# A graph network's edge stages: TensorE's results one or two steps further from their readers, and its semaphore increments moved from matmuls to drains

## The chip, the cores and the metric

The kernel runs on one core of one Trainium2 chip. The metric is the device time of one execution in microseconds (us). The core has five engines with a queue each: TensorE (PE: matmuls and the weight loads before them), VectorE (DVE), ScalarE (ACT), GpSimd (POOL, which here issues the gathers) and SyncE (SP, which issues the other DMAs). The engines meet through semaphores: an instruction adds to one, and another waits until it has reached a number.

## The reference

A node table of 12,500 rows of 128 floats, 200,000 edges with `src` (random) and `dst` (sorted), and 16 attributes for each edge. In short:

```
h  = relu(layernorm(x))
logit = tanh(h @ W1.T) @ w2                       # one number a node
x1 = x + segment_softmax_sum(logit[src], h[src])  # the pooling: softmax over the edges of each dst
h  = relu(layernorm(x1))
y  = relu(transformer_conv(h, 8 heads of 16))     # the multi-head stage
out = x1 + transformer_conv(y, 1 head of 128)     # the single-head stage
transformer_conv: q[dst] . (k[src] + edge_attr @ We), softmax over the edges of each dst,
                  sum of weight * (v[src] + edge_attr @ We), plus x @ Ws + bs
```

## The kernel before

The edges are cut into 391 blocks of 512 (four columns of 128), the nodes into 98 tiles of 128. An *item* is a block with one tile that its `dst` values touch; there are 488 items, since some blocks touch several tiles. Three edge stages run over all items, one after the other: "pool" (`dense_stage`, L1060), "multi" (`edge_stage`, L661) and "single" (`dense_stage` again). Between them are short stages over nodes.

In each edge stage GpSimd gathers the source rows of a block by four indirect DMAs (L1133, or L752 in multi) into a ring of blocks and waits until a slot has been read. Each other engine runs its own program, `step(n, u)` for n = 0, 1, ..., which `rolled` (L67) writes out in full. Within a step an engine works on items that lie back by a fixed number: `m1 = n - 1`, `m2 = n - 2` and so on. These numbers, the order of the pieces in each `step`, and the waits are all that sets the order of the work.

The chain of one item in the two dense stages, with the names of its semaphores: ScalarE copies the gathered rows out of the ring (`rows`); in single, TensorE turns them (`rowT`) and ScalarE copies the result (`rowT_sb`); TensorE makes the scores in PSUM (`score`); VectorE masks them and takes the running minimum (`low`); ScalarE makes `exp` of them (`prob`) and of the change of the minimum (`factor`); TensorE turns the probabilities (`probT`); VectorE copies them to SBUF (`probT_sb`); TensorE multiplies them with the rows (`partial`); VectorE adds that to the tile's sums (`summed`). In pool, TensorE also makes the edge terms of the multi stage for each of the 391 blocks (`term_made`), and ScalarE copies them (`term_copied`). Each of TensorE's results there has two PSUM buffers.

In multi, TensorE has seven groups of matmuls in each step, each with its semaphore: `alphaT` (L911), `partial` (L924 and L926), `prefix` (L931), `edge_max` (L937 and L939), `onehotT` (L945), `tile_max` (L953) and `query` (L962). The chain of one item passes TensorE three times in one step: `alphaT`, the scan on VectorE, `prefix`, `ends` on VectorE, `tile_max`.

Every group of matmuls ends in one increment, which hangs on its last matmul (`i.then_inc(...)`).

## Time and profile before

| | |
|---|---|
| median of 3 runs | 9990.61 us (9988.7 to 9993.93) |
| the profiled execution, first to last instruction | 10223.7 us |
| mean granted clock of TensorE in it | 0.744 |
| busy: PE, DVE, ACT, POOL | 67%, 45%, 35%, 45% |
| pool, multi, single | windows 213 to 3195, 3464 to 6790, 6917 to 10118 us |

The profiled execution is one of its own and 233 us (2.3%) longer than the median of the others. PE is the engine's matmuls, PEld its weight loads, which run beside matmuls. A granted clock of 1.0 means that TensorE ran at 2.4 GHz, 0.5 that it ran at 1.2 GHz; a number between is a mix over the stretch. The modelled end of a matmul in such a profile doesn't tell when its semaphore arrives: for that one reads when the waiting engine starts. "Remote" as the releaser of a wait means that no instruction of the profile ended within 1.5 us before the semaphore moved. The chain that ended last, in the page's own count, covers only the last node stage and tells nothing of the edge stages.

### The profile page before, as it was taken

To read this page: it belongs to the slowest core of one execution; us is meant where nothing else is said; L and a number is where in the kernel's file an instruction comes from. 1 tells how busy PE (TensorE), PEld (TensorE's weight loads), DVE (VectorE), ACT (ScalarE), POOL (GpSimd) and SP (SyncE) were. 2 spreads that over 40 slices of the span, in tenths; PEclk is the share of its full clock that TensorE was granted. 3 is DMA by queue.
4 is the path that set the end of the run, shared out by engine and by line. 5 is a ranking of instruction groups with operands and counts; after the bars stand their busy time and mean duration, and the time that the engine had idled before them with its cause. 6 is when DMAs were issued, how large, how long until landed. Compare 5 with 4: busy or idle time off the path is not lost. (4 is left out here: it accounts for less than half of the span.)

```text
span 10223.7 us, 177251 instructions
## 1 busy us (share of the span) xinstructions
PE 6865.3 (67%) x40779; PEld 5286.7 (52%) x40779; DVE 4586.4 (45%) x12423; ACT 3560.6 (35%) x8557; POOL 4600.9 (45%) x4738
## 2 busy tenths in 40 slices
PE   3667666687655555555566666676777778778787
PEld 2556656576544345555555555553444444444445
DVE  3233333333346555566666666662333333333333
ACT  2233333333323344444444444442222323233332
POOL 2555544444441355544444444425544444444441
PEclk6666667767777677777777777787777878888888
DMA  2333333343322544444444444443333333333332
GB/s 77 95 102 103 101 102 105 105 109 107 94 59 80 151 136 137 136 138 138 135 136 136 137 137 141 136 141 74 76 75 76 77 74 76 74 75 75 73 75 62
DMA packets 1085568, 1056.97 MB, mean 103 GB/s; under 512 B 398824, under 2 KB 857244, under 8 KB 1084532
## 3 DMA queue, kind: packets, MB, share of 16 engines
q1 hardware_dynamic: 909364, 633.73, 22.8%
q0 software_dynamic: 175168, 411.90, 15.6%
q8 instruction: 349, 5.72, 0.2%
q14 instruction: 687, 5.63, 0.2%
HBM read 885.97 MB, written 159.07 MB: 102 GB/s over the span
## 5 line engine op out<-in xcount | busy, mean ns | idle before, releaser
L752 POOL DMA_INDIRECT ring_multi<-kv_rows,src_cols x1564 | 1606.5, 1027 | 1766.8 <-DVE kv L837 1205.8
L1133 POOL DMA_INDIRECT ring_single<-h_rows,src_cols x1564 | 1476.4, 944 | 1688.9 <-ACT row_single L1301 1180.6
L1133 POOL DMA_INDIRECT ring_pool<-pool_rows,src_cols x1564 | 1476.6, 944 | 1609.7 <-ACT row_pool L1301 1000.8
L1262 PE MATMUL ps_p_pool<-row_pool,probT_pool 128*128 128x129 f32 x3904 | 798.3, 369 | 998.8 <-DVE probT_pool L1226 924.9
L1262 PEld LDWEIGHTS ps_p_pool<-row_pool,probT_pool 128*128 128x128 f32 x3904 | 707.5, 271 | 1074.9 <-DVE probT_pool L1226 990.3
L1306 ACT ACTIVATE rowT<-ps_r 128x512 f32<-128x512 f32 x488 | 291.3, 597 | 2190.6 <-remote 1216.2
L1242 PE MATMUL ps_s_single<-rowT,cols 128*128 128x512 f32 x976 | 657.1, 762 | 465.2 <-issue 393.4
L1262 PE MATMUL ps_p_single<-row_single,probT_single 128*128 128x145 f32 x3904 | 737.9, 344 | 219.0 <-DVE probT_single L1226 181.0
L1213 DVE CUSTOM_DVE_ANT_0 masked_single<-mask_single,ps_s_single,start_single 128x512 f32<-128x512 bf16 x488 | 364.9, 748 | 986.4 <-PE ps_s_single L1244 524.7
L1262 PEld LDWEIGHTS ps_p_single<-row_single,probT_single 128*128 128x128 f32 x3904 | 663.5, 238 | 248.1 <-DVE probT_single L1226 202.8
L924 PE MATMUL ps_p_multi<-message_multi,onehot 128*128 128x136 f32 x3904 | 751.6, 354 | 4.8 <-issue 4.8
L1213 DVE CUSTOM_DVE_ANT_0 masked_pool<-mask_pool,ps_s_pool,start_pool 128x512 f32<-128x512 bf16 x488 | 365.0, 748 | 831.9 <-remote 408.5
L931 PE MATMUL ps_f_multi<-ident,prefix_multi 36*128 36x36 f32 x488 | 136.7, 280 | 880.9 <-DVE prefix_multi L847 633.2
L924 PEld LDWEIGHTS ps_p_multi<-message_multi,onehot 128*128 128x128 f32 x3904 | 704.4, 262 | 4.2 <-issue 4.2
L1010 ACT ACTIVATE onehot<-onehot_multi 128x512 f32<-128x512 bf16 x488 | 307.3, 630 | 1139.7 <-remote 863.1
L1292 ACT ACTIVATE prob_pool<-masked_pool,low_pool 128x512 f32<-128x512 f32 x488 | 352.2, 722 | 939.1 <-DVE low_pool L1213 617.8
L837 DVE TENSOR_TENSOR kv<-ring_multi,term_multi 128x1024 f32<-128x1024 f32 x488 | 598.5, 1226 | 157.6 <-issue 149.4
L1244 PE MATMUL ps_s_single<-edge_tail,cols_tail 17*128 17x512 f32 x976 | 663.5, 764 | 0.0
L1312 ACT ACTIVATE edge_term<-ps_e_pool 128x512 f32<-128x512 f32 x391 | 231.4, 592 | 1111.4 <-remote 663.4
L1278 PE MATMUL ps_e_pool<-w_edge,attr_cols 16*128 16x128 f32 x3128 | 583.5, 339 | 10.2 <-DMA attr_cols<-in_edge_cols 10.2
L931 PEld LDWEIGHTS ps_f_multi<-ident,prefix_multi 36*128 36x128 f32 x488 | 75.7, 155 | 985.2 <-DVE prefix_multi L847 682.5
L1278 PEld LDWEIGHTS ps_e_pool<-w_edge,attr_cols 16*128 16x128 f32 x3128 | 495.7, 237 | 113.0 <-issue 113.0
(224 smaller groups left out, 13519.3 us busy)
## 6 DMA issues: line engine op xcount, KB each, us to landing
term_multi<-edge_terms SPq DMA_DIRECT2D x488, 256.0 KB
edge_terms<-edge_term SPq DMA_DIRECT2D x391, 256.0 KB
dst_pool<-in_dst_rows SPq DMA_DIRECT2D x488, 128.0 KB
dst_multi<-in_dst_rows SPq DMA_DIRECT2D x488, 128.0 KB
dst_single<-in_dst_rows SPq DMA_DIRECT2D x488, 128.0 KB
query_multi<-query_parts SPq DMA_DIRECT2D x488, 96.0 KB
cols<-query_cols SPq DMA_DIRECT2D x488, 64.0 KB
ring_pool<-pool_rows,src_cols POOLq DMA_INDIRECT x1564
```

What stands on the lines that cost most here:

```text
L752: pool.indirect_dma_start(out=ring[:, u, j, :], out_offset=None, in_=rows, in_offset=bass.IndirectOffsetOnAxis(ap=g.src_cols[:, c:c + 1], ...
L837: V.tensor_tensor(out=kv[:, u1 % 4], in0=in_ring(items.block(m1), 0, 2 * D).rearrange("p j (a c) -> p j a c", a=2), in1=term[:, m1 % EB].u ...
L924: T_.matmul(ps_p[:, 0:acc_w], lhs, rhs, start=(j == 0), stop=False)
L1010: S_.activation(onehot32[:, p3], onehot[:, m3 % OB], ACT.Copy).then_inc(E["onehot32"].sem, 1)
L1133: pool.indirect_dma_start(out=ring[:, u, j, :], out_offset=None, in_=rows, in_offset=bass.IndirectOffsetOnAxis(ap=g.src_cols[:, c:c + 1], ...
L1213: V.tensor_tensor_reduce(out=masked[:, p], in0=mask[:, p], in1=ps_s[p][:], scale=1.0, scalar=start[:, p], op0=ALU.add, op1=ALU.min, accum_ ...
L1242: T_.matmul(ps_s[p1][:], cols[:, u1 % QB], rowT[:, p1], start=True, stop=False)
L1244: T_.matmul(ps_s[p1][:], cols_tail[:, u1 % QB], edge_tail[:, u1], start=False, stop=True)\
L1262: i = T_.matmul(ps_p[p3][:, 0:acc_w], probT[:, p3, j], row[:, u3, j, 0:acc_w], start=(j == 0), stop=(j == J - 1))
L1278: i = T_.matmul(ps_e[n % 2][:, j * D:(j + 1) * D], attr[:, n % EB, j * P:(j + 1) * P], w_edge[:], start=True, stop=True)
L1292: S_.activation(prob[:, p2], masked[:, p2], ACT.Exp, bias=low[:, p2], scale=-1.0)\
L1306: S_.activation(rowT[:, u % 2], ps_r[u % 2][:], ACT.Copy).then_inc(E["rowT_sb"].sem, 1)
```

## The change

1. All increments of TensorE in the three edge stages leave the last matmul of their group and go to a `drain` instruction behind it. A drain waits in TensorE's queue until the engine has finished all that came before; then it increments.
2. In the pool stage the product `partial` moves from TensorE's step n - 3 to n - 5 and `probT` from n - 2 to n - 3; VectorE reads them at n - 4 and n - 2 instead of n - 2 and n - 1. In single, TensorE's pieces but `rowT` move one step further still (`late = 1`): `score` at n - 2, `probT` at n - 4, `partial` at n - 6, and ScalarE's `exp` at n - 3.
3. ScalarE copies the gathered rows one item ahead, ahead of its `exp`, and in single the turned rows one item back. `factor` has 8 buffers instead of 4.

The core of the diff; in multi the other six groups are changed as the one shown:

```diff
-                    T_.matmul(ps_p[:, 0:acc_w], g.ident[:], kept_sums[:, p5], start=False, stop=True)\
-                      .then_inc(E["partial"].sem, 1)
+                    T_.matmul(ps_p[:, 0:acc_w], g.ident[:], kept_sums[:, p5], start=False, stop=True)
+                    pe.drain().then_inc(E["partial"].sem, 1)
...
+    late = 1 if single else 0
...
-        factor = sb(g, ph, f"factor_{kind}", [P, 4, 1])
+        factor = sb(g, ph, f"factor_{kind}", [P, U, 1])
...
         @block.vector
-                m1, u1, p1 = n - 1, (u - 1) % U, (u - 1) % 2
-                m2, p2, f2 = n - 2, u % 2, (u - 2) % 4
+                m2, p2 = n - 2, u % 2
+                m4, p4, f4 = n - 4, u % 2, (u - 4) % U
...
+                if has(m4, ITEMS):
+                    E["partial"].wait(dve, m4)
+                    E["factor"].wait(dve, m4)
...
+                    E["probT"].wait(dve, m2)
+                    E["partial"].wait(dve, m2 - 2)
+                    V.tensor_copy(probT[:, p2].rearrange("p j n -> p (j n)"), ps_t[p2][:])\
...
         @block.tensor
-                m1, u1, p1 = n - 1, (u - 1) % U, (u - 1) % 2
-                m2, p2 = n - 2, u % 2
-                m3, u3, p3 = n - 3, (u - 3) % U, (u - 3) % 2
+                m1, u1, p1 = n - 1 - late, (u - 1 - late) % U, (u - 1 - late) % 2
+                m3, p3 = n - 3 - late, (u - 3 - late) % 2
+                m5, u5, p5 = n - 5 - late, (u - 5 - late) % U, (u - 5 - late) % 2
...
+                if has(m5, ITEMS):
+                    E["probT_sb"].wait(pe, m5)
+                    E["summed"].wait(pe, m5 - 2)
...
+                    pe.drain().then_inc(E["partial"].sem, 1)
                 if has(m3, ITEMS):
...
+                    E["prob"].wait(pe, m3)
+                    E["probT_sb"].wait(pe, m3 - 2)
...
+                    pe.drain().then_inc(E["probT"].sem, 1)
...
         @block.scalar
+                k, r = n + 1, n - 1
+                m2, p2, f2 = n - 2 - late, (u - 2 - late) % 2, (u - 2 - late) % U
...
+                if n == 0:
+                    rows_of_item(0, 0)
+                if has(k, ITEMS):
+                    rows_of_item(k, 1)
+                if single and has(r, ITEMS):
+                    E["rowT"].wait(act, r)
```

The distances show at the start of a stage, where the pieces come in one by one. TensorE at the start of the pool stage, before (`ps_e` is the edge terms, `ps_s` the scores, `ps_t` the turned probabilities, `ps_p` the product):

```order
L1278 MATMUL ps_e_pool<-w_edge,attr_cols 128x128 x4
L1249 MATMUL ps_s_pool<-ident,row_pool 128x128 x4
L1278 MATMUL ps_e_pool<-w_edge,attr_cols 128x128 x4
L1249 MATMUL ps_s_pool<-ident,row_pool 128x128 x4
L1269 MATMUL ps_t_pool<-ident,prob_pool 128x128 x4
L1278 MATMUL ps_e_pool<-w_edge,attr_cols 128x128 x4
L1249 MATMUL ps_s_pool<-ident,row_pool 128x128 x4
L1262 MATMUL ps_p_pool<-row_pool,probT_pool 128x129 x4
L1269 MATMUL ps_t_pool<-ident,prob_pool 128x128 x4
```

Two scores stand ahead of the first turn, and the first product comes one step behind that turn. The same place after the change:

```order
L1280 MATMUL ps_e_pool<-w_edge,attr_cols 128x128 x4
L1251 MATMUL ps_s_pool<-ident,row_pool 128x128 x4
L1280 MATMUL ps_e_pool<-w_edge,attr_cols 128x128 x4
L1251 MATMUL ps_s_pool<-ident,row_pool 128x128 x4
L1271 MATMUL ps_t_pool<-ident,prob_pool 128x128 x4
L1280 MATMUL ps_e_pool<-w_edge,attr_cols 128x128 x4
L1251 MATMUL ps_s_pool<-ident,row_pool 128x128 x4
L1271 MATMUL ps_t_pool<-ident,prob_pool 128x128 x4
L1280 MATMUL ps_e_pool<-w_edge,attr_cols 128x128 x4
L1251 MATMUL ps_s_pool<-ident,row_pool 128x128 x4
L1264 MATMUL ps_p_pool<-row_pool,probT_pool 128x129 x4
L1271 MATMUL ps_t_pool<-ident,prob_pool 128x128 x4
```

Three scores stand ahead of the first turn, and the first product comes two steps behind it; within a step, once all pieces run, the order is the old one. (Drains are not among such rows.) ScalarE at the start of the single stage, before (rows that only compute addresses stand between):

```order
L1301 ACTIVATE row_single<-ring_single 128x4x128
L1306 ACTIVATE rowT<-ps_r 128x512
L1292 ACTIVATE prob_single<-masked_single,low_single 128x512
L1295 ACTIVATE factor_single<-start_single,low_single 128x1
L1299 REGISTER_ALU x2
```

This is its third step: the row copy, the turned rows of the same item, and then the first `exp` (the start of the next step's work). The first turned rows after the change:

```order
L1298 ACTIVATE row_single<-ring_single 128x4x128
L1308 ACTIVATE rowT<-ps_r 128x512
L1296 REGISTER_ALU x2
L1296 ISA
L1298 REGISTER_ALU
```

Here the row copy is that of an item two ahead of the turned rows beside it, and no `exp` comes yet: the first one stands two row copies further on.

## Rows read from the trace of the kernel before

**Rows 1.** Busy time in the three edge stages and in 17 us of pool.

```profile
core 0: us, PE busy (x) PEld busy (x) DVE busy (x) ACT busy (x) POOL busy (x), PEclk, DMA share, GB/s
213.00:3195.00 2982.00, 1974.91 (x10908) 1736.36 (x10908) 1051.85 (x2923) 922.51 (x1855) 1469.73 (x1557) 0.69 0.36 96
3464.00:6790.00 3326.00, 1993.86 (x18437) 1786.18 (x18434) 2092.89 (x5340) 1468.69 (x4370) 1574.78 (x1533) 0.73 0.48 136
6917.00:10118.00 3201.00, 2516.88 (x9756) 1505.05 (x9755) 1058.60 (x2926) 948.84 (x1950) 1468.00 (x1556) 0.80 0.32 74
1392.60:1409.80 17.20, 4.90 (x39) 4.08 (x36) 2.48 (x8) 3.36 (x7) 11.29 (x12) 0.70 0.37 92
```

**Rows 2.** Waits of PE in pool: total us, times, longest.

```profile
PE ps_p_pool L1262 <- DVE probT_pool L1226: 922.8, 208, 32.4
```

**Rows 3.** Waits of PE in multi, same columns.

```profile
PE ps_f_multi L931 <- DVE prefix_multi L847: 612.2, 203, 10.5
PE ps_m_multi L953 <- DVE ends_multi L893: 343.4, 151, 8.6
```

**Rows 4.** Waits of PE in single, same columns.

```profile
PE ps_s_single L1242 <- issue: 393.4, 121, 18.0
PE ps_p_single L1262 <- DVE probT_single L1226: 181.0, 80, 8.6
```

**Rows 5.** Timeline of pool: start us, us, engine, line, operation, idle before it.

```profile
1395.23 0.60 PE L1269 MATMUL ps_t_pool<-ident,prob_pool 128*128 128x128 f32 x4
...
1395.76 1.15 PE L1278 MATMUL ps_e_pool<-w_edge,attr_cols 16*128 16x128 f32 x8
...
1397.82 0.08 DVE L1213 DVE_READ_ACCUMULATOR2_ANT low_pool<- 128x1 f32 x1
1397.94 0.72 ACT L1292 ACTIVATE prob_pool<-masked_pool,low_pool 128x512 f32<-128x512 f32 x1 [3.38 <-issue]
...
1406.30 0.94 POOL L1133 DMA_INDIRECT ring_pool<-pool_rows,src_cols  x1 [0.30 <-issue]
1409.78 0.69 DVE L1226 COPY probT_pool<-ps_t_pool 128x512 f32<-128x512 f32 x1 [4.51 <-remote]
...
1409.87 0.60 ACT L1312 ACTIVATE edge_term<-ps_e_pool 128x512 f32<-128x512 f32 x1 [10.50 <-remote]
...
1410.52 1.87 PE L1262 MATMUL ps_p_pool<-row_pool,probT_pool 128*128 128x129 f32 x7 [13.03 <-DVE probT_pool L1226]
```

**Rows 6.** Groups by line, POOL in pool: busy us, mean ns, idle before.

```profile
L1133 POOL DMA_INDIRECT ring_pool<-pool_rows,src_cols x1557 | 1469.9, 944 | 1473.7 <-ACT row_pool L1301 1000.8 <-issue 467.4 <-DMA ring_pool<-pool_rows,src_cols 5.5
```

**Rows 7.** One step of each stage at either clock; columns of rows 1.

```profile
1447.32:1452.94 5.62, 5.62 (x25) 5.06 (x24) 1.83 (x5) 2.03 (x4) 4.40 (x5) 0.50 0.44 116
1508.66:1511.65 2.99, 2.99 (x25) 2.71 (x24) 2.04 (x6) 0.81 (x2) 0.00 (x0) 0.99 0.17 51
8499.12:8505.72 6.60, 6.60 (x20) 4.18 (x19) 2.44 (x9) 3.34 (x7) 3.39 (x4) 0.51 0.39 87
8509.80:8513.73 3.93, 3.93 (x22) 2.41 (x21) 2.16 (x7) 2.12 (x6) 1.89 (x2) 1.00 0.40 87
5023.10:5028.10 5.00, 5.00 (x42) 4.68 (x41) 4.52 (x12) 3.05 (x9) 1.50 (x2) 0.53 0.28 65
5001.37:5005.83 4.46, 3.13 (x42) 2.71 (x40) 4.12 (x12) 2.94 (x12) 1.47 (x2) 1.00 0.48 144
```

**Rows 8.** Timeline of PE in pool at 1.2 GHz.

```profile
1444.45 2.09 PE L1262 MATMUL ps_p_pool<-row_pool,probT_pool 128*128 128x129 f32 x8 [3.17 <-DVE probT_pool L1226]
1446.33 1.06 PE L1269 MATMUL ps_t_pool<-ident,prob_pool 128*128 128x128 f32 x4
1447.32 2.07 PE L1278 MATMUL ps_e_pool<-w_edge,attr_cols 16*128 16x128 f32 x8
1449.32 1.11 PE L1249 MATMUL ps_s_pool<-ident,row_pool 128*128 128x128 f32 x4
1450.23 0.64 PE L1262 MATMUL ps_p_pool<-row_pool,probT_pool 128*128 128x129 f32 x2
```

**Rows 9.** Timeline of PE in pool at 2.4 GHz.

```profile
1509.74 0.65 PE L1249 MATMUL ps_s_pool<-ident,row_pool 128*128 128x128 f32 x4
1510.23 1.06 PE L1262 MATMUL ps_p_pool<-row_pool,probT_pool 128*128 128x129 f32 x8
1511.13 0.60 PE L1269 MATMUL ps_t_pool<-ident,prob_pool 128*128 128x128 f32 x4
```

More of the change, by code:

```diff
@@ L952, in step @@
                     for j in range(J):
-                        i = T_.matmul(tile_max[:, j], onehot[:, m2 % OB, j], ends[:, p2, j], start=True, stop=True)
-                    i.then_inc(E["tile_max"].sem, 1)
+                        T_.matmul(tile_max[:, j], onehot[:, m2 % OB, j], ends[:, p2, j], start=True, stop=True)
+                    pe.drain().then_inc(E["tile_max"].sem, 1)
                 if not pool_k and has(n, ITEMS):
@@ L1243, in step @@
                         landed(pe, g.attrs_loaded, attrs_base, m1, u1, 32)
-                        T_.matmul(ps_s[p1][:], cols_tail[:, u1 % QB], edge_tail[:, u1], start=False, stop=True)\
-                          .then_inc(E["score"].sem, 1)
+                        T_.matmul(ps_s[p1][:], cols_tail[:, u1 % QB], edge_tail[:, u1], start=False, stop=True)
+                        pe.drain().then_inc(E["score"].sem, 1)
                     else:
@@ L1293, in step @@
                       .then_inc(E["prob"].sem, 1)
-                    E["summed"].wait(act, m2 - 4)
+                    E["summed"].wait(act, m2 - U)
                     S_.activation(factor[:, f2], start[:, p2], ACT.Exp, bias=low[:, p2], scale=-1.0)\
                       .then_inc(E["factor"].sem, 1)
-                if has(n, ITEMS):
-                    E["partial"].wait(act, n - U)
-                    act.wait_ge(blocks_ready, items.block(u) + (1 + blocks_base))
-                    settle(g, act)
-                    S_.activation(row[:, u, :, 0:copied], in_ring(items, u, 0, copied), ACT.Copy)\
-                      .then_inc(E["rows"].sem, 1)
-                    if single:
-                        E["rowT"].wait(act, n)
-                        E["score"].wait(act, n - 2)
-                        S_.activation(rowT[:, u % 2], ps_r[u % 2][:], ACT.Copy).then_inc(E["rowT_sb"].sem, 1)
                 k = n - 1
@@ L1312, in step @@
                     S_.activation(term[:, k % EB], ps_e[k % 2][:], ACT.Copy).then_inc(term_copied, 1)
[L1313 removed]
+            rolled(act, ITEMS, U, 2 + late, step, items.begin)
     for k in DENSE_SIGNALS:
```

84 lines of the change are left out of this document (39 added, 45 removed).

## The prediction

> **What bounds the kernel now.** Busy time by stage comes first. TensorE works 1975 of 2982 us in pool, 1994 of 3326 in multi and 2517 of 3201 in single [rows 1]. It stands for 1007, 1332 and 684 us: 3023 us in all, and more than half of the time that it works passes at 1.2 GHz (granted clock 0.69, 0.73, 0.80). No other engine does more: VectorE is at 63% in multi at most, and GpSimd, 49% busy in pool, itself waits 1001 us there for ScalarE to free a ring slot [rows 6]. By the table of waits TensorE waits for VectorE: in pool for the copied probabilities (923 us, 208 times) [rows 2], in multi for `prefix` and `ends` [rows 3], in single for `probT_sb`, and 393 us under "issue", for which the view has no releaser [rows 4].
>
> The timeline says what VectorE waits for. The matmuls of `probT` start at 1395.23 and should be done at 1395.83. VectorE, idle for 4.51 us, starts the copy that needs them at 1409.78, 13.9 us late. The matmuls of the edge terms should end at 1396.91, and ScalarE, idle for 10.50 us, reads them at 1409.87. TensorE's next product, which needs the copy, follows at 1410.52 after 13.03 us of idleness [rows 5]. The two results are 1.1 us apart in TensorE's queue and reach their readers 0.09 us apart. Had the matmuls been late, the second group would have needed its 1.1 us after the first. So the work was done, and it is the increments that were held. In the same stretch VectorE's increment at 1397.90 released ScalarE at 1397.94: others aren't held. What else happens there is a run of gathers: 12 in 17.2 us [rows 1], the last ending at 1407.24 [rows 5]. After that the readers start. My reading: while GpSimd's gathers run, increments that hang on matmuls arrive microseconds late. That, and not work, is most of TensorE's 3023 us, and the low clock follows it: TensorE runs at 1.2 GHz after it has stood.
>
> The Trainium skill (PSUM — Partial Sum Buffer, Engine vs sequencer instructions) says that an update on the matmul fires when the instruction completes, and that a drain waits for the engine to go fully idle. The trace doesn't bear out the first for the time of arrival (13.9 us). By the page's rule a drain can't be the faster messenger; this is the first rival below.
>
> **The change part by part.** *Increments on drains.* There are 1855 drains in pool (3 x 488 + 391), 3416 in multi (7 x 488) and 1952 in single (4 x 488): 7223. No drain with an increment stands in the stages of before, so its price is bounded. Behind it in TensorE's queue stand the next group's weight loads and matmuls, which now start on an empty engine. What is lost is the overlap of two groups. At 1.2 GHz `ps_t` begins 0.21 us before `ps_p` ends (1446.33 against 1446.54), `ps_e` and `ps_s` 0.07 before their forerunners; eight matmuls that start on an idle engine take 2.09 us, against 1.93 in a stream [rows 8]. That is 0.14 + 0.16 = 0.30 us. At 2.4 GHz the overlaps are 0.16 [rows 9], and with half the restart it is about 0.20. Handling of the drain itself is added to that; I take 0.27 us for one, 0.20 to 0.50 as bounds (the upper one if handling costs as much as the rest). That makes 501, 922 and 527 us, together 1950 (bounds 1445 to 3612).
>
> By the Trainium skill (TensorE: Matmul & The Clock Gate, Single matmul latency) the fixed part of a matmul's latency is 166 to 183 ns. An estimate by that page for 7223 exposed latencies is 1.2 to 1.3 ms; the rows above have the restart as well.
>
> *Do drains arrive in time?* If the held thing is the matmul's own message, a drain, which TensorE's sequencer sends, passes by it. If TensorE's messages as a whole are held, a drain is held too, and then it blocks what stands behind it. Rows 5 show the matmuls done while the message is out, and TensorE taking its own waits on time; so I take the first, at about 4 to 1.
>
> *Two steps of room* (pool and single). Before, TensorE's step p needs VectorE's copy of item p - 3 from VectorE's step p - 2, which needs `score` from TensorE's step p - 1: each late increment stops both at once. After, TensorE's step p needs only VectorE's step p - 3 (`probT_sb` of p - 5, `low` of p - 3), so one increment may be a whole step late at no cost. The order rows show the distance; the matmuls are the same in number. ScalarE's row copy one item ahead frees ring slots sooner, against GpSimd's wait of 1001 us [rows 6]. That wait goes anyway when ScalarE is no longer held. The extra register loads and moved pieces lie on ScalarE, 31% busy in pool and 30% in single: nothing. No DMA is added, and SyncE's program is untouched.
>
> *What goes.* With increments in time and room, TensorE's idleness falls to what is real. In multi there is 4.46 - 3.13 = 1.33 us in a step at 2.4 GHz in which TensorE waits for VectorE with nothing held [rows 7]; the drains' 7 x 0.27 us partly fill it, and I leave 350 us. In pool I leave 150 (start, ring), in single 100. Gone: 857 + 982 + 584 = 2423.
>
> *The clock.* The share of time at 1.2 GHz is 2 x (1 - granted): 0.62, 0.54, 0.40. A step costs 5.62 us low and 2.99 high in pool, 5.00 and 3.13 of work in multi, 6.60 and 3.93 in single [rows 7]. With few stalls I take shares of 0.35, 0.40 and 0.20. Pool: (2.99 + 2.63 x 0.35) / (2.99 + 2.63 x 0.62) = 0.846 of 1975, so 304 saved; multi 0.937 of 1994, 126; single 0.893 of 2517, 269. Together 699. Multi gets least, since seven drains in a step leave TensorE gappy.
>
> *Sum.* -2423 + 1950 - 699 = -1172 us: pool -660, multi -186, single -326. The profiled execution (10223.7 us) would take 9052; taken off the median of 9990.6, that is **8820 us**. Next late is TensorE itself with its drains in single and multi, and in pool GpSimd: 1564 gathers x (0.94 + 0.30) us = 1940 us.
>
> **The rivals.**
>
> *Drains are held as well* (slower). TensorE then stands at each drain while gathers run. For it: the page's rule, and that nothing in this trace shows a drain getting through. Against it: rows 5, as above. Price: work and drains 8436 us (6486 + 1950), and half of GpSimd's 1940 us in each of three stages, 2910: 11346 against 9509, so +1837 and about 11830 us. It decides if a drain's message comes as late as the matmul's.
>
> *The clock stays low* (slower). The drains arrive in time, but their gaps keep TensorE at 1.2 GHz. For it: the low share is already 0.4 to 0.62. Against: the clock fell after stalls of microseconds, and 4.46 us steps of multi with 1.33 us idle ran at 1.00 [rows 7]. Price: 2402 + 2408 + 3322 of work, 2167 of drains (at 0.30), 600 idle: 10899, so +1390 and 11380 us. The gain is used up where the low share rises a quarter of the way from before to 1 (0.72, 0.66, 0.55).
>
> *Drains cost what they save* (slower or same). The late increments are only half of the idleness, and the gathers (a ring waits for its landings) the rest. Then half of 1007 and 684 goes through the room, and in multi half of 1332, against 1950 of drains with the clock as before: -1512 + 1950 = +438, about 10430 us; with drains at 0.20, even. Against it: in rows 1 DMA is at 32 to 48%.
>
> *The clock stays high.* All stalls gone and no step at 1.2 GHz: work 1278 + 1508 + 1978, drains at 0.25 us 1806, multi's 350 idle; pool can't go below GpSimd's 1940. 1940 + 2712 + 2466 = 7118 against 9509: -2391 and 7600 us.
>
> **How the numbers follow.** Forecast 0.53, its own range 8100 to 9700 (drain at 0.20 to 0.40 us, low shares as before to half of mine). Clock high 0.12, clock low 0.11, drains held 0.14, cost what they save 0.10. A change under 0.2% (20 us) can't be told from none here. Faster: 0.53 + 0.12 = 0.65. Same: 0.03, slower 0.07 of the fifth case; with 0.11 and 0.14 slower is 0.32. The range runs from 7500 to 11000; outside are most of the held drains, half of the clock-low case and a little of the clock-high one, 0.2.
>
> **What would show it.** Right: in the same views VectorE's copies and ScalarE's `term` reads start within 0.3 us of the drained group's end, also in runs of 8 or 12 gathers; "remote" goes from VectorE's and ScalarE's waits; GpSimd's wait for ring slots falls well below 1001 us; groups of TensorE stand 0.2 to 0.35 us further apart; the granted clock rises above 0.8 in pool and single, and less in multi. Wrong: gaps of 5 us or more on TensorE right behind a drain while gathers run (drains held); a granted clock below 0.65 with few gaps (clock low); single or multi longer than before while pool is shorter (the drains' price is over 0.5 us).

## The result, and the profile after

The changed kernel takes 11959.59 us (median of 3, 11946.39 to 11996.01) against 9990.61: ratio 1.1975 (95% interval 1.194 to 1.2009). It is slower, and outside the range of 7500 to 11000 us. Its profiled execution spans 11944.6 us. The mean granted clock is 0.622 (0.744 before).

Busy time by stage in the changed kernel, as in [rows 1]:

```profile
core 0: us, PE busy (x) PEld busy (x) DVE busy (x) ACT busy (x) POOL busy (x), PEclk, DMA share, GB/s
210.00:3532.00 3322.00, 2601.12 (x10928) 2050.24 (x10928) 1075.59 (x2925) 939.73 (x1854) 1481.72 (x1558) 0.57 0.32 86
3754.00:8012.00 4258.00, 3042.92 (x18544) 2426.40 (x18544) 2158.01 (x5368) 1494.37 (x4392) 1552.43 (x1559) 0.50 0.38 108
8145.00:11841.00 3696.00, 2866.08 (x9752) 1541.15 (x9752) 1078.72 (x2925) 943.09 (x1949) 1463.57 (x1550) 0.78 0.28 64
```

The window of multi in [rows 1] begins at 3464 us, 42 us behind that stage's first matmul. From 3422 on, as counted here, multi took 3368 us before. So pool is 336 us longer, multi 890, single 496. TensorE's idleness fell only from 3054 to 2766 us (721 + 1215 + 830), while its busy time rose from 6501 to 8510 us for the same matmuls. The clock tells a part of that: 0.69 became 0.57, multi stands at 0.50 from end to end, and single went from 0.80 to 0.78.

The timeline of pool in the changed kernel, the place that answers to [rows 5, 8]:

```profile
1502.29 0.69 DVE L1228 COPY probT_pool<-ps_t_pool 128x512 f32<-128x512 f32 x1 [0.69 <-issue]
...
1502.46 2.04 PE L1280 MATMUL ps_e_pool<-w_edge,attr_cols 16*128 16x128 f32 x8 [0.23 <-issue]
...
1504.56 0.60 ACT L1322 ACTIVATE edge_term<-ps_e_pool 128x512 f32<-128x512 f32 x1 [1.30 <-issue]
...
1504.73 1.09 PE L1251 MATMUL ps_s_pool<-ident,row_pool 128*128 128x128 f32 x4 [0.23 <-issue]
...
1506.05 2.06 PE L1264 MATMUL ps_p_pool<-row_pool,probT_pool 128*128 128x129 f32 x8 [0.23 <-issue]
...
1507.71 0.94 POOL L1135 DMA_INDIRECT ring_pool<-pool_rows,src_cols  x1 [0.30 <-issue]
...
1508.33 1.08 PE L1271 MATMUL ps_t_pool<-ident,prob_pool 128*128 128x128 f32 x4 [0.23 <-issue]
...
1508.96 0.95 POOL L1135 DMA_INDIRECT ring_pool<-pool_rows,src_cols  x1 [0.30 <-issue]
1509.48 0.69 DVE L1228 COPY probT_pool<-ps_t_pool 128x512 f32<-128x512 f32 x1 [0.69 <-PEq L1272]
...
1509.65 0.76 PE L1280 MATMUL ps_e_pool<-w_edge,attr_cols 16*128 16x128 f32 x2 [0.23 <-issue]
```

Two things stand here. In this step the messages are prompt: the last turn ends at 1509.41 and VectorE copies at 1509.48, inside a run of gathers, where before it was 13.9 us. And every group starts 0.23 us after the modelled end of the one ahead, where before it started 0.07 to 0.21 us ahead of that end. The step is 7.19 us (1502.46 to 1509.65), against 5.62 at the same clock [rows 7].

Not every drain gets through at once. Most end 0.02 us after the modelled end of their group, and their increments move 0.01 us behind that. But 960 of the 7223 (10% in pool, 14% in multi and in single) end over 0.3 us after it, 1001 us too late in all, and TensorE stands meanwhile. Of these, 13 end over 5 us late, 12 of them at the start of a stage, where GpSimd fills the ring in long runs of gathers. The longest:

```profile
223.05 2.04 PE L1280 MATMUL ps_e_pool<-w_edge,attr_cols 16*128 16x128 f32 x8 [7.72 <-issue]
...
244.30 0.94 POOL L1135 DMA_INDIRECT ring_pool<-pool_rows,src_cols  x1 [0.30 <-issue]
...
244.57 0.60 ACT L1322 ACTIVATE edge_term<-ps_e_pool 128x512 f32<-128x512 f32 x1 [14.57 <-PEq L1282]
...
244.74 1.08 PE L1251 MATMUL ps_s_pool<-ident,row_pool 128*128 128x128 f32 x4 [19.65 <-issue]
```

The edge terms end at 225.09, and the drain behind them at 244.53. No matmul of this stage carries an increment in this kernel.

GpSimd's line in pool, as [rows 6], shows that the wait for a ring slot didn't fall but rose from 1001 to 1284 us, since the consumers are slower:

```profile
L1135 POOL DMA_INDIRECT ring_pool<-pool_rows,src_cols x1564 | 1488.2, 952 | 1903.5 <-ACT row_pool L1298 1284.1 <-issue 483.9 <-POOLq L409 133.4
```

### The profile page after: what moved, and what is told of

The parts are those of the page before. It is cut to its first block and busy times, and to the rows that moved or that the text cites. A ratio compares the mean times of both kernels' runs of the same rounds, so it can differ in the third digit from the quotient of the medians.

```text
span 11944.6 us, 184714 instructions
## 1 busy us (share of the span) xinstructions
PE 8869.5 (74%) x40779; PEld 6261.0 (52%) x40779; DVE 4681.4 (39%) x12423; ACT 3587.8 (30%) x8557; POOL 4564.8 (38%) x4738
## 5 line engine op out<-in xcount | busy, mean ns | idle before, releaser
L925 PE MATMUL ps_p_multi<-message_multi,onehot 128*128 128x136 f32 x3904 | 1049.4, 450 | 112.0 <-issue 111.2
L1298 ACT ACTIVATE row_single<-ring_single 128x512 f32 x488 | 308.4, 632 | 2645.8 <-PEq L1266 2175.9
L1264 PE MATMUL ps_p_pool<-row_pool,probT_pool 128*128 128x129 f32 x3904 | 931.1, 413 | 197.6 <-issue 197.4
L925 PEld LDWEIGHTS ps_p_multi<-message_multi,onehot 128*128 128x128 f32 x3904 | 907.4, 330 | 241.7 <-issue 241.7
L1264 PEld LDWEIGHTS ps_p_pool<-row_pool,probT_pool 128*128 128x128 f32 x3904 | 805.2, 305 | 356.8 <-issue 347.8
L963 PE MATMUL ps_q_multi<-query_multi,onehotT_multi 128*128 128x128 bf16 x5856 | 702.0, 309 | 332.0 <-issue 332.0
L1280 PE MATMUL ps_e_pool<-w_edge,attr_cols 16*128 16x128 f32 x3128 | 698.7, 390 | 138.6 <-issue 128.2
L963 PEld LDWEIGHTS ps_q_multi<-query_multi,onehotT_multi 128*128 128x128 bf16 x5856 | 586.1, 142 | 361.8 <-issue 361.8
L1280 PEld LDWEIGHTS ps_e_pool<-w_edge,attr_cols 16*128 16x128 f32 x3128 | 606.1, 285 | 279.6 <-issue 279.6
L1271 PE MATMUL ps_t_pool<-ident,prob_pool 128*128 128x128 f32 x1952 | 505.3, 410 | 202.8 <-issue 202.7
```

Of the source, the lines that this page charges most:

```text
L925: T_.matmul(ps_p[:, 0:acc_w], lhs, rhs, start=(j == 0), stop=False)
L963: T_.matmul(ps_q[:, j], onehotT[:, n % OB, j], query[:, u % QB, k, 0:D], start=(k == 0), stop=(k == 2))
L1264: T_.matmul(ps_p[p5][:, 0:acc_w], probT[:, p5, j], row[:, u5, j, 0:acc_w], start=(j == 0), stop=(j == J - 1))
L1271: T_.transpose(ps_t[p3][:, j * P:(j + 1) * P], prob[:, p3, j * P:(j + 1) * P], g.ident[:])
L1280: T_.matmul(ps_e[n % 2][:, j * D:(j + 1) * D], attr[:, n % EB, j * P:(j + 1) * P], w_edge[:], start=True, stop=True)
```

## The experiments

In the table a stage's time goes from its first matmul (in pool and single, its first scores) to its last one in the profiled execution. "Late" is the share of the increments that hang on matmuls that arrive over 0.3 us after the modelled end of their matmul, with the mean lateness of all in us: both are worked out by pairing each move of a semaphore in the trace with its matmul. With indirect gathers the trace has 65 to 100% of the moves, so the shares are of those. Ratios are to runs of the kernel before on the same chip, with 95% intervals; rows without one have a single run. Beside these rows the kernel before took 9987, 10005, 10176, 10196, 10016 and 10184 us in six sets of runs, so two times from different sets can be up to 2% apart with nothing to explain.

| kernel | us | ratio | pool / multi / single | clock | late in pool, multi, single |
|---|---|---|---|---|---|
| before | 9990.6 | | 2986 / 3368 / 3200 | 0.744 | .55 .45 .48 (2.5, 1.6, 1.7) |
| after | 11959.6 | 1.1975 (1.194 to 1.2009) | 3322 / 4258 / 3696 | 0.622 | none on matmuls |
| room only | 9340.5 | 0.9344 (0.9322 to 0.9366) | 2692 / 3245 / 2775 | 0.769 | .64 .48 .60 |
| drains only | 11863.7 | 1.1882 (1.1855 to 1.191) | 3316 / 4256 / 3607 | 0.633 | none on matmuls |
| room, plain drains | 11905.2 | | 3289 / 4220 / 3721 | 0.621 | .11 .15 .14 (0.2) |
| room, one drain a step, before a wait | 10230.4 | 1.0222 (1.0185 to 1.0258) | 2988 / 3275 / 3302 | 0.736 | .39 .41 .33 |
| room, one drain a step, elsewhere | 10223.8 | | 3022 / 3329 / 3195 | 0.753 | .34 .42 .35 |
| room, two or three drains | 11005.2 | | 3155 / 3698 / 3479 | 0.673 | .25 .20 .24 |
| before, rows by plain DMA | 6338.1 | | 1550 / 2194 / 1929 | 0.922 | 0 0 0 (0.01) |
| before, gathers of rows in order | 9959.5 | | 2929 / 3227 / 3140 | 0.754 | .54 .47 .48 |
| room, rows by plain DMA | 6330.0 | | 1538 / 2194 / 1924 | 0.922 | 0 0 0 (0.01) |
| drains, rows by plain DMA | 9864.5 | | 2566 / 3905 / 2733 | 0.717 | none on matmuls |
| more room | 9474.4 | 0.9298 (0.9271 to 0.9325) | 2652 / 3325 / 2824 | 0.764 | .67 .46 .60 (3.0, 1.6, 2.0) |
| room, gathers with GpSimd drains | 20744.6 | 2.0365 (2.03 to 2.043) | 6400 / 7012 / 6575 | 0.595 | 0 0 0 (0.01) |
| more room, a memset behind each gather | 9745.1 | 0.9564 (0.9542 to 0.9587) | 2931 / 3206 / 2943 | 0.739 | .04 .12 .08 (0.05, 0.17, 0.08) |
| more room, three memsets | 12242.3 | | 3768 / 4024 / 3755 | 0.664 | 0 .02 0 (0.01, 0.03, 0.01) |
| more room, a GpSimd drain each block | 10787.6 | 1.0587 (1.0562 to 1.0613) | 3226 / 3665 / 3236 | 0.723 | .15 .32 .15 (0.2, 0.4, 0.2) |
| more room, a memset each second gather | 8645.4 | 0.8639 (0.8608 to 0.8671) | 2563 / 2819 / 2583 | 0.788 | .24 .56 .26 (0.3, 1.0, 0.4) |
| more room, memsets in multi alone | 9272.6 | 0.9259 (0.9228 to 0.9289) | 2625 / 3199 / 2786 | 0.766 | .66 .10 .61 |
| before, a memset each second gather | 8711.9 | 0.8554 (0.8525 to 0.8582) | 2597 / 2859 / 2592 | 0.792 | .26 .56 .36 (0.4, 1.0, 0.5) |

### The parts of the change

**Room only**: the changed kernel with all increments back on the last matmul.

```diff
-                    pe.drain().then_inc(E["partial"].sem, 1)
+                    i.then_inc(E["partial"].sem, 1)
```

> The changed kernel with all 13 kinds of increment back on the last matmul: the two steps of room alone, and multi as before. Theory A (the loss is the drains' gaps and the low clock that follows them; the room itself helps): pool and single shorter than before, since one held increment no longer stops both engines: I expect pool 2982 to about 2500 us and single 3201 to about 2900, multi unchanged at 3370, together 9200 us (9000 to 9500). Rival B (the room costs as well, because held increments or ring slots come later in the longer chain): pool and single not shorter than before, 9950 to 10300 us. Increments are still held: readers microseconds late in runs of gathers.

It is 6.6% faster than the kernel before, within what theory A had expected (9000 to 9500). By the profiled executions pool is 294 us shorter and single 425, although increments come as late as ever. Multi, whose program is that of before, is 123 us shorter in the same pair: the profiled execution of the kernel before was 2.3% over its median, so some 120 us of each may be no gain of the room.

**Drains only**: the kernel before with all 13 kinds of increments on drains.

> The kernel before with all 13 kinds of increment on drains, and none of the room. Theory A: the drains are the loss. Multi is then as in the changed kernel (4258 us, clock 0.50), and pool and single lose more than there, since their short chain now has the drain's latency in every step and nothing to hide it: pool 3500, single 4000, together 12400 us (12000 to 13000). Rival B (the room is part of the loss): pool and single shorter than in the changed kernel (3322 and 3696), together under 11900 us.

It is about as slow as the changed kernel (11864 against 11960). Theory A's 12000 to 13000 us was missed: without room the drains cost no more. Pool and multi are as in the changed kernel, and single is 89 us shorter. With drains the room gives nothing, and by the ratios (1.1882 and 1.1975) it costs a little.

**Plain drains**: the version with room, increments on matmuls, and a drain without increment behind each.

```diff
                     i.then_inc(E["score"].sem, 1)
+                    pe.drain()
```

> The room with the increments on the matmuls, and a drain without an increment behind each group: the drains' gaps without their timely messages. If a drain waits only for the array (theory A), it ends about 0.02 us after the last matmul also while that matmul's increment is held, gaps between groups are 0.23 us as in the changed kernel, and the increments are still held, so it is slower than the changed kernel: about 12500 to 13500 us. If a drain counts a held increment as unfinished work (rival C), TensorE stands behind it for microseconds in runs of gathers, and the time goes to 14000 us or more.

Neither theory had this: the time is the changed kernel's (one run), so it is the drain that costs and not its message. And the matmul's own increment now comes in time as a rule: the late share falls from .64, .48, .60 to .11, .15, .14. The drains themselves end over 0.3 us late at .10, .14, .14, the same shares as in the changed kernel. So an increment on the matmul, with a drain behind it, is late about as seldom as the drain.

### The price of a drain

**One drain in each step, ahead of a wait** (behind `score` in pool, `probT` in single, `partial` in multi), plain, on the version with room:

> The room, all increments on matmuls, and one plain drain in a step, where TensorE is about to wait anyway: behind the score in pool, behind probT in single, behind partial in multi. Theory D (a drain lets the increments before it out, whatever hangs on it, and one in a step is enough): few increments late, little price: pool 488 x 4.5 to 5, multi x 5.5, single x 4.8, together 7900 to 8500 us. Rival E (what frees them is a pause behind each group, so one drain frees only its own group): late shares near those without drains, 9200 to 9600 us. Rival F: the drain stands while increments are out: 10000 us or more.

**One drain elsewhere** (behind `partial` in pool and single, `onehotT` in multi), and **two** (`score`, `probT`) **in pool and single and three** (`partial`, `onehotT`, `query`) **in multi**:

> As the run with one drain where TensorE waits, but at another place: behind partial in pool and single, behind onehotT in multi. By theory D the place matters little beyond 0.4 us a step of gap: within 400 us of that run. By rival E the group with the drain has its increment in time and the others are late; in pool and single the time is 9200 to 9600 us in all.

> The room, increments on matmuls, two plain drains in a step of pool and single (behind score and probT), three in multi (partial, onehotT, query). By theory D nothing more is freed and each drain more costs 0.4 to 0.55 us and clock: 300 to 700 us over the run with one drain. By rival E the time falls with each drain's group or stays, 9000 to 9800 us. In multi it tells how many drains the 2.4 GHz clock bears: with one it should be granted in part, with seven it never was; three lies between.

The first drain costs pool and single far more than a quarter of what four cost: pool 2692, 2988, 3155, 3289 with none, one, two and all; single 2775, 3302, 3479, 3721. Multi goes 3245, 3275, 3698, 4220 with none, one, three, seven. Its place hardly matters (10230 and 10224 us). The forecast of theory D (7900 to 8500 us with one drain) failed, and rival F (a drain that stands while increments are out) fits. The timeline of pool with one drain (behind `ps_s`) shows why a few drains are dear:

```profile
1500.98 0.65 PE L1249 MATMUL ps_s_pool<-ident,row_pool 128*128 128x128 f32 x4
...
1502.53 0.94 POOL L1133 DMA_INDIRECT ring_pool<-pool_rows,src_cols  x1 [0.30 <-issue]
...
1505.18 0.60 ACT L1322 ACTIVATE edge_term<-ps_e_pool 128x512 f32<-128x512 f32 x1 [3.34 <-remote]
1505.45 0.75 DVE L1213 CUSTOM_DVE_ANT_0 masked_pool<-mask_pool,ps_s_pool,start_pool 128x512 f32<-128x512 bf16 x1 [2.72 <-remote]
...
1505.49 2.06 PE L1263 MATMUL ps_p_pool<-row_pool,probT_pool 128*128 128x129 f32 x8 [3.86 <-issue]
```

The scores end at 1501.63. Their increment and that of `ps_e` are held until 1505.2 to 1505.4, and TensorE, with no wait of its own named, starts its next product with them. The drain is held as the increments are. With one drain a step .45, .44, .49 of the drains end over 0.3 us late; with two or three .26, .32, .32; with one behind every group .10, .14, .14. The shares of late increments fall in the same way (table). Why more drains leave less held was not tested.

**Drains with nothing held**: the kernel before with plain DMAs for the gathers (this leaves out the gather by `src`), without and with drains.

```diff
-                    pool.indirect_dma_start(
-                        out=ring[:, u, j, :], out_offset=None, in_=rows,
-                        in_offset=bass.IndirectOffsetOnAxis(ap=g.src_cols[:, c:c + 1], axis=0),
-                    ).then_inc(gathered[n % 2][j], 16)
+                    pool.dma_start(ring[:, u, j, :], rows[(c % NODE_TILES) * P:(c % NODE_TILES + 1) * P, :])\
+                        .then_inc(gathered[n % 2][j], 16)
```

> The kernel before with the gathers replaced by plain DMAs of GpSimd of 128 rows that follow one another in the table: same count, bytes and ring, wrong rows (the gather by src is left out). Theory: what holds TensorE's increments is the indirect gather itself (its descriptors made by GpSimd's software). Then the increments arrive within 0.02 us here, and the time falls to what a step costs at 2.4 GHz: pool 488 x 3.2, multi x 4.5, single x 4.0, or GpSimd's own rate, together 6500 to 7500 us. Rival: any DMA traffic of GpSimd's queue into the ring holds them: increments late as before, 9500 to 10500 us.

> The kernel before with plain DMAs of consecutive rows (leaves out the gather by src) and all of TensorE's increments in the three stages on drains. Nothing is held, so this is the drains' price alone, against 6338 us. Theory A (the price is the exposed latency, 0.2 to 0.4 us a drain at the high clock, and the clock stays high without long stalls): pool 1550 + 1855 x 0.3 = 2100, multi 2194 + 3416 x 0.4 = 3560, single 1929 + 1952 x 0.4 = 2700; total about 9000, granted clock above 0.9 in pool and single. Theory B (drains alone bring the low clock): steps of 7.1, 9.0 and 9.4 us as with drains and gathers, pool 3300, multi 4250, single 3600, total about 11800, granted clock below 0.65.

Busy time by stage with plain DMAs, without drains:

```profile
208.00:1760.00 1552.00, 1423.80 (x10928) 1276.16 (x10928) 1051.20 (x2926) 897.57 (x1856) 831.51 (x1557) 0.96 0.63 184
1985.00:4180.00 2195.00, 1748.70 (x18529) 1557.86 (x18528) 2018.21 (x5370) 1459.95 (x4391) 827.37 (x1553) 0.87 0.69 208
4310.00:6240.00 1930.00, 1922.57 (x9773) 1182.55 (x9772) 1053.34 (x2929) 943.68 (x1949) 821.99 (x1547) 1.00 0.50 123
```

and with drains:

```profile
208.00:2774.00 2566.00, 2125.30 (x10927) 1673.29 (x10928) 1069.95 (x2925) 931.98 (x1854) 831.73 (x1557) 0.74 0.38 111
2998.00:6903.00 3905.00, 3041.93 (x18544) 2424.72 (x18544) 2157.61 (x5368) 1493.07 (x4390) 822.59 (x1553) 0.50 0.39 117
7026.00:9759.00 2733.00, 2268.92 (x9756) 1208.59 (x9755) 1078.11 (x2925) 938.41 (x1950) 821.92 (x1553) 1.00 0.35 87
```

Drains alone cost 3526 us. Single shows the bare price, since its clock is 1.00 in both: 803 us for 1952 drains, **0.41 us each**. In pool and multi the drains also take the clock from 0.96 to 0.74 and from 0.87 to 0.50, and a drain comes to 0.55 and 0.50 us. Of the two theories each holds in a part: the clock stays up in single, and falls to the floor in multi. One step of single, timeline of TensorE with plain DMAs and drains:

```profile
8004.38 0.63 PE L1253 MATMUL ps_r<-ident,row_single 128*128 128x128 f32 x4 [0.26 <-issue]
...
8009.93 0.63 PE L1253 MATMUL ps_r<-ident,row_single 128*128 128x128 f32 x4 [0.23 <-issue]
8010.79 1.23 PE L1259 MATMUL ps_p_single<-row_single,probT_single 128*128 128x145 f32 x8 [0.23 <-issue]
8012.25 0.63 PE L1266 MATMUL ps_t_single<-ident,prob_single 128*128 128x128 f32 x4 [0.23 <-issue]
```

and without drains, where groups overlap:

```profile
5000.41 0.66 PE L1252 MATMUL ps_r<-ident,row_single 128*128 128x128 f32 x4
5000.90 1.16 PE L1258 MATMUL ps_p_single<-row_single,probT_single 128*128 128x145 f32 x8
5001.90 0.60 PE L1265 MATMUL ps_t_single<-ident,prob_single 128*128 128x128 f32 x4
```

The step is 5.55 us against 3.93 [rows 7]: 1.62 us for four drains. Of each 0.41, 0.23 is the gap and 0.17 the overlap that is gone (`ps_p` used to start 0.17 us ahead of the modelled end of `ps_r`, 5000.90 against 5001.07).

### What holds an increment

**Indirect gathers with rows in order**: the kernel before, its indices replaced by an iota that names consecutive rows (this leaves out `src`).

```diff
+            pool.iota(src_cols[:], pattern=[[7, BLOCKS * J]], base=0, channel_multiplier=1)
```

> The kernel before with its indirect gathers kept, but with indices that name 128 rows in a row (the reference's src is left out, so the rows are wrong). It tells the indirect instruction from the scattered addresses. If the instruction holds TensorE's increments (descriptors made by GpSimd's software), they are late as before and the time stays at 9800 to 10000 us. If scattered reads of HBM do it, the increments arrive at once and the time falls to 6300 to 7000 us.

It takes 9959 us and has the late shares of the kernel before. So scattered addresses are not the cause; the indirect instruction is, since with plain DMAs of the same bytes on the same engine not one increment is late, and the kernel takes 6338 us. Not all of the 3650 us is the holds' price: a plain DMA also takes less of GpSimd's time (832 us of pool instead of 1470).

**Room with plain DMAs** (leaves out the gather by `src`):

> The version with room only, with the gathers replaced by plain DMAs of 128 consecutive rows (leaves out the gather by src). Nothing is held then. Theory A (room is worth only what held increments cost): the same as the kernel before with that replacement, 6338 us within 1%, pool 1550, multi 2194, single 1929. Theory B (room takes away waits of the chain itself too): pool or single 3% shorter or more, total below 6200.

6330 against 6338 us: room is worth only what held increments cost.

**More room**: `late = 1` in pool too, which makes it three steps.

> The version with room only (all increments on matmuls), with pool's pieces of TensorE one step further still, as single has them (late = 1 in both). Theory A (held increments are paid for only where they outlast the room): pool, 2692 us with two steps of room, gets 50 to 250 us shorter; multi 3245 and single 2775 stay within 1%; total 9100 to 9300. Theory B (what is left of pool is the low clock and GpSimd's ring, and distance is worth nothing more): pool within 1.5% of 2692, total 9300 to 9400.

Pool is 40 us shorter (theory A wanted at least 50), but single, with the same code as in the version with room, is 49 us longer, and the total of 9474 us lies above both forecasts, in a set of slower runs. So one execution can't tell this last piece of distance from nothing.

### Ending the hold on GpSimd's side

**Memsets with GpSimd's drain behind each gather**, on the version with room:

```diff
                     ).then_inc(gathered[n % 2][j], 16)
+                    for _ in range(2): pool.memset(idle[:], 0.0); pool.drain()
```

> The version with room only, with two memsets of 128x128 on GpSimd (each followed by GpSimd's own drain) behind each gather, so that gathers stand some 0.5 to 0.8 us further apart. GpSimd then has 1564 x (0.94 + 0.3 + 0.6) = about 2900 us in each stage. Theory A (an increment is held only while a gather instruction runs and gets through in the pause behind it): late increments come at most 1 us late, the granted clock rises above 0.85, multi falls from 3245 to below 3000, pool and single are bound by GpSimd at 2800 to 3000; total 8700 to 9200. Theory B (the hold lasts as long as gathers follow each other at any such distance, or belongs to what the gathers have queued): late increments stay at half or more, stages are longer than with room only by what GpSimd adds, total above 9500.

Theory A missed the time by a factor of two, and was right on the increments: next to none is late. Theory B had only "above 9500" for the time and was wrong on the increments. The timeline of GpSimd shows the price, 1.44 us of idleness behind the first memset and 0.96 behind the second:

```profile
3000.19 0.95 POOL L1135 DMA_INDIRECT ring_pool<-pool_rows,src_cols  x1 [0.75 <-issue]
3001.15 0.22 POOL L1139 MEMSET idle_pool<- 128x128 f32 x1
3002.81 0.20 POOL L1139 MEMSET idle_pool<- 128x128 f32 x1 [1.44 <-issue]
3003.97 0.95 POOL L1135 DMA_INDIRECT ring_pool<-pool_rows,src_cols  x1 [0.96 <-issue]
```

**One and three memsets behind each gather**, each waited for by its semaphore instead of a drain, and **one GpSimd drain a block**, on the version with more room:

```diff
+        pool.memset(idle[:], 0.0).then_inc(g.paced, 1)
+        pool.wait_ge(g.paced, g.paces)
```

> The version with more room (increments on matmuls), with one memset of 128x128 on GpSimd behind each gather, and GpSimd waiting for its semaphore: a pause of some 0.3 to 0.5 us, without GpSimd's drain. Theory A (any pause between two gathers lets the held increments through): late increments fall below 0.2, none over 1.5 us late, GpSimd has 1564 x (0.94 + 0.3 + 0.4) = 2560 us in each stage; total 8300 to 9100. Theory B (it was the length of the pause, 3 us, or GpSimd's drain that freed them): the late share stays over 0.4 and the mean hold gets longer with the bursts; total 9400 to 10000.

> As the short pause, with three memsets behind each gather, each waited for: about 1.0 to 1.3 us of pause. GpSimd then has 1564 x (0.94 + 0.3 + 1.1) = 3700 us a stage, which bounds pool and single. If the length of the pause decides, increments that the short pause leaves late are prompt here (late share below 0.1) and the total is near 3 x 3700 = 11100; if GpSimd's drain decides, they are late here too (over 0.4) and the total is above 11500.

> The version with more room, with one drain of GpSimd behind every fourth gather. The drain takes about 1.5 us, so GpSimd has 1564 x 1.24 + 391 x 1.5 = 2530 us a stage. Theory A (the hold ends at GpSimd's drain or the pause behind it): no increment is over 5.5 us late, the mean lateness falls below 1.5 us in pool (3.0 now); total 8700 to 9300. Theory B (shorter bursts change nothing, since a step is 3 to 6 us long and four gathers already outlast it): within 2% of 9474 or slower by what GpSimd adds.

One memset of 0.22 us is enough to end most holds; the longest left is 2.8 us, in multi (theory A had none over 1.5). The timeline of GpSimd with it:

```profile
1499.42 0.95 POOL L1143 DMA_INDIRECT ring_pool<-pool_rows,src_cols  x1 [1.35 <-ACT row_pool L1306]
1500.38 0.22 POOL L94 MEMSET idle_pool<- 128x128 f32 x1
1500.87 0.95 POOL L1143 DMA_INDIRECT ring_pool<-pool_rows,src_cols  x1 [0.27 <-issue]
...
1506.82 0.95 POOL L1143 DMA_INDIRECT ring_pool<-pool_rows,src_cols  x1 [1.34 <-issue]
```

From one gather's end to the next one's start it is now 0.49 us instead of 0.30, and the late share in pool falls from .67 to .04. But the kernel is slower than with more room alone: a block takes GpSimd 7.40 us (1499.42 to 1506.82), and 391 of them are 2893 of pool's 2931 us. GpSimd has become the bound, and TensorE waits for it at the low clock. My sum had 2560 us a stage, since it left out the 1.3 us at the head of each block. Three memsets leave nothing late in pool and single at still more cost (12242 us, where about 11100 was expected), so it is not GpSimd's drain that is needed. A GpSimd drain once a block makes holds short too but leaves GpSimd idle for 3 to 4 us each time, twice what I had expected, and is slower than the kernel before: 10788 us for 8700 to 9300.

**A memset behind every second gather**, and **memsets in multi alone**:

```diff
+                    if j % 2: pace(g, pool, idle, 1)
```

> The version with more room, with the short pause (one memset, waited for) behind every second gather only. Theory A (a hold lasts to the next pause, so pairs of gathers hold an increment 2 us at most, which the room covers, and GpSimd pays half as much as with a pause behind each): pool 2550 to 2750, multi 3100 to 3250, single 2650 to 2850, total 9100 to 9400. Theory B (the chip's loss is GpSimd's time and the low clock and no longer the holds): between the two, 9474 and 9745.

> The version with more room, with the short pause behind each gather in the multi stage alone, the only stage without room. If the stages are independent, it is the sum of parts already measured: pool 2652, multi 3206 for 3325, single 2824, total 9474 - 119 = 9355 (9300 to 9400). If a stage's pace carries over to the next, single differs from 2824 by over 2%.

The first is the better: 8645 us, below its forecast of 9100 to 9400. Increments are still late at one in four or two, but by 1.0 to 1.5 us in the median instead of 3 to 4. The second gives the sum of its parts or a little less: 9273 us, just under the 9300 to 9400 expected, with multi at 3199 for 3325 (3206 was expected).

**The same pause without room**, on the kernel before:

> The kernel before (no room, all increments on matmuls) with the short pause behind every second gather. Theory A (pause and room cover the same loss: a hold of at most 2 us costs little even without room in pool and single): multi as in e20 (2819), pool and single within 5% of e20 (2563 and 2583), total 8600 to 8950. Theory B (without room each hold of 1 to 2 us still stops the chain): pool 2750 to 2950, single 2800 to 3050, total 9000 to 9500.

8711.9 us, ratio 0.8554 (0.8525 to 0.8582): the pause alone gives all of the gain, and room adds nothing that can be told (8645 us but a ratio of 0.8639 with it, on another chip). It is the best ratio of all kernels that keep the gather by `src`, 14% faster than the kernel before and some 27% than the changed one (8711.9 / 11959.6 = 0.728, over two sets of runs). Its busy time by stage:

```profile
213.00:2810.00 2597.00, 1980.40 (x10928) 1769.69 (x10927) 1059.73 (x2926) 890.47 (x1854) 1650.96 (x2336) 0.72 0.41 110
3033.00:5892.00 2859.00, 2045.38 (x18544) 1821.44 (x18544) 2097.48 (x5368) 1473.55 (x4391) 1832.09 (x2339) 0.76 0.56 160
6019.00:8611.00 2592.00, 2176.01 (x9755) 1340.00 (x9756) 1055.86 (x2925) 980.82 (x1951) 1648.96 (x2335) 0.90 0.40 92
```

And GpSimd's timeline in it:

```profile
1500.12 0.95 POOL L1144 DMA_INDIRECT ring_pool<-pool_rows,src_cols  x1 [1.54 <-issue]
1501.37 0.94 POOL L1144 DMA_INDIRECT ring_pool<-pool_rows,src_cols  x1 [0.31 <-issue]
1502.32 0.22 POOL L94 MEMSET idle_pool<- 128x128 f32 x1
...
1506.64 0.95 POOL L1144 DMA_INDIRECT ring_pool<-pool_rows,src_cols  x1 [1.42 <-issue]
```

A block is 6.52 us here, 391 of them 2549 of pool's 2597: GpSimd bounds pool and single, and the next thing to shorten is its own 1.5 us at the head of a block.

## Why the prediction was wrong

The forecast was -1172 us in the three stages of the profiled execution. Counted alike on both sides they are 1722 us longer: 2894 us apart. (By the medians the kernel is 1969 us longer; the profiled execution of the kernel before was 233 us over its median.) Three terms of the sum failed, and one piece of the mechanism.

**That drains pass by the hold** was wrong, though it looked right at most places. That TensorE's increments are held while gathers run is borne out. But I had argued that a drain, sent by the sequencer, passes by what is held. The runs with one drain a step have it late about as often as an increment, and in the changed kernel 13% of the drains are late although no matmul before them carries an increment. So the rival "drains are held as well" (chance 0.14) was true in part: its sign, gaps of 5 us or more right behind a drain while gathers run, came 13 times. It was wrong in its price: drains late by 1001 us in all, not 2910. With plain DMAs for the gathers no drain ends over 0.14 us late.

**"What goes"** (2423 us) was over by some 475 us. The changed kernel's idleness of 2766 us holds 7223 gaps of 0.23 us, 1661 us; 1105 us remain where I had left 600. Nearly all of it, 1001 us, is the lateness of drains, for which I had booked nothing. The 600 us that I had kept for real waits were not there.

**The price of a drain** failed: 0.27 us taken, 0.41 measured at a constant clock (0.39 at the low one, (7.19 - 5.62) / 4). I had the lost overlap (0.14 to 0.16 us), which was about right, but took for the rest what eight matmuls from a standing start take longer than in a stream, half of it at 2.4 GHz. The 1.93 us of the stream stand in no line of rows 8, but in this one:

```profile
1450.23 1.93 PE L1262 MATMUL ps_p_pool<-row_pool,probT_pool 128*128 128x129 f32 x8
```

By the rows the start is worth little: the four groups of a step of pool take 6.27 us together with drains and 6.17 without. What a drain costs besides the overlap is that the next group starts 0.23 us late at either clock. Multiplied out it is 1661 us of gaps and 7223 x 0.16 = 1156 us of overlap, 2817 for 1950: 867 us. By the Trainium skill (TensorE: Matmul & The Clock Gate, Single matmul latency) the fixed latency is 166 to 183 ns; the measured gap is 0.23 us, so the estimate by that page was too low as well.

**The clock** failed most, and in its sign. I let the share of time at 1.2 GHz fall to 0.35, 0.40 and 0.20 because the stalls would go. By the granted clock it rose to 0.86, 1.00 and 0.44. Of the 2009 us of added busy time 1156 are lost overlap and 853 the clock, where I had -699: 1552 us. This split is an estimate. The steps of rows 7 with the new shares give the clock 740 us, and the overlaps that the trace of the kernel before really has add up to 836 us, which would leave it 1173. The sign is the same in each. My argument was that stalls of microseconds bring the clock down. The run with drains and nothing held refutes that this is the only way: its longest gap within a stage is 1.7 us, and multi stands at 0.50 throughout. That was the rival "the clock stays low", with a chance of 0.11 and 11380 us; with drains at 0.41 instead of 0.30 it gives 11380 + 7223 x 0.11 = 12175, and the changed kernel took 11960. That it comes so near is in part luck: it has single at 1.2 GHz throughout, where the measured share is 0.44, and nothing for late drains. My point against it, that multi ran at 1.00 with 1.33 us idle in a step of 4.46 [rows 7], was another pattern of idleness than seven gaps in each step.

475 + 867 + 1552 = 2894 us. Had the clock stayed as it was, the change would still have been about +1722 - 853 = +870 us (550 to 980 by the other two splits).

**The room** was credited jointly with the drains. The runs split them: with increments on matmuls room is worth 6.6%, with drains nothing, with nothing held nothing (6330 and 6338 us). Room lets a message be late, and a drain pays for it not to be: two cures for one loss, and I had booked the dearer of the two as needed.

**What stays open.** Why a run of indirect gathers holds what TensorE sends was not found, nor was it tried whether in the short pause the other instruction counts or the 0.2 us more between two gathers. By the Trainium skill (Perfetto Trace Analysis, DMA Instruction — SWDGE (GPSIMD)) the profile's end of such a DMA is the last descriptor written and not the end of its work. The idleness of 1.44 us that GpSimd's drain shows behind a gather and a memset agrees; it doesn't say what the tail is. By the Trainium skill (Perfetto Trace Analysis, Per-engine timelines) a matmul's update goes out when PSUM has acknowledged the write. The trace has no row for that. With plain DMAs the update follows the modelled end by 14 ns on average; with gathers the trace can't tell a late acknowledgement from a held message. Drains that are late with no increment before them fit the first, but no run here decides it.

## What to carry to other kernels

Before paying for another messenger, ask whether it passes by the hold, and take away what holds the first one: here one memset of 0.22 us between pairs of gathers gave 14.5%, where drains took 20%. Price a drain on TensorE by the start of the next group as well as the lost overlap (0.4 us here), count them per step, and don't book a clock gain for removed stalls while adding gaps to every group. And when a change holds two cures for one loss, run each alone.

## What had not been expected of the hardware

- TensorE's increments, and only those (VectorE's arrive within about 10 ns), come microseconds late while GpSimd's indirect DMAs follow each other 0.30 us apart; at 0.49 us, with a memset between, 4 to 12% of them are over 0.3 us late instead of 46 to 67%.
- An indirect gather holds GpSimd for 944 ns, a plain DMA of as many rows for about 540, and replacing the first by the second takes the kernel from 9990 to 6338 us, which is more than the engines' busy times in the kernel before let one guess.
- A drain on TensorE costs 0.41 us at a constant clock. It is held by runs of indirect gathers as an increment is, up to 19.4 us, also where no matmul before it carries an increment.
- Seven drains in a step of multi keep the granted clock at 0.50 for 3905 us with nothing held; four in a step of single leave it at 1.00.
- GpSimd stands idle for about 1 to 4 us at a drain of its own behind gathers.
